# Masked sums of the encoder with the total taken out of row 0 of the value tables, in three jobs instead of four

## The reference, cut to what matters

```
smask = (i[:, None] & i[None, :] == 0)          # 1024 x 1024, 0 or 1
scores = einsum('bhqd,bhkd->bhqk', q, k) * scale
scores = scores * smask                         # masked scores are 0, not -inf
a = softmax(scores, axis=-1)
att = einsum('bhqk,bhkd->bhqd', a, v)
h = _ln(h + att @ wo + bo_, g1, be1)
h = _ln(h + gelu(h @ w1 + b1_) @ w2 + b2_, g2, be2)
```

## Time and profile before

| What | Value |
|---|---|
| median of 3 runs | 1929.28 us |
| the profiled execution | 1931.52 us, span of its instructions 1929.7 us |
| busy: PE, DVE, ACT, POOL | 1637.2, 1410.2, 1199.9, 254.4 us |
| mean granted clock of TensorE | 0.94 |
| chain that ended last: PE, DVE, ACT, issue, DMA | 38, 11, 8, 5, 4% |
| of it: DMA emr<-sce (the read-back of the maxima) | 4% |

### The profile page before, as it was taken

The page is one execution under the profiler, slowest core; times in us unless marked ns, Lnnn a source line. Parts: engine busy times, 40 slices in busy tenths (PEclk is TensorE's granted clock), DMA queues, the critical chain, the costliest instruction groups (busy, mean ns, idle before and its releaser), DMA issues.

```text
span 1929.7 us, 67065 instructions
## 1 busy us (share of the span) xinstructions
PE 1637.2 (85%) x28905; PEld 908.7 (47%) x28905; DVE 1410.2 (73%) x3361; ACT 1199.9 (62%) x2142; POOL 254.4 (13%) x229
## 2 busy tenths in 40 slices
PE   2789999899857689898989888888889898988896
PEld 1123333233324355555556555555555555656554
DVE  7778888987668767676867768576767686776755
ACT  2047776677831466676766767666766676776652
POOL 1000000000010202020302112120302030301111
PEclk8569999999977799999999999999999999999998
DMA  6122102001023433325242432343333424243000
GB/s 150 25 51 80 39 3 51 2 3 27 1 57 78 120 89 74 87 66 133 54 119 53 126 73 82 67 118 68 74 98 81 108 54 119 54 133 66 6 8 17
DMA packets 152204, 130.83 MB, mean 68 GB/s; under 512 B 65013, under 2 KB 147381, under 8 KB 149893
## 3 DMA queue, kind: packets, MB, share of 16 engines
q1 hardware_dynamic: 134629, 125.75, 26.6%
q10 hardware_dynamic: 17280, 0.79, 0.6%
HBM read 79.25 MB, written 45.88 MB: 65 GB/s over the span
## 4 chain that ended last, share of the span: by engine, by line
PE 38%; DVE 11%; ACT 8%; issue 5%; DMA 4%; ACTq 1%; POOL 0%; POOLq 0%; DVEq 0%
PE pB L670 8%; PE pO L685 7%; PE pA L650 6%; PE pG L621 5%; PE pG L631 5%; DMA emr<-sce 4%; DVE mx L933 3%; ACT PB L795 3%; PE pG L566 2%; ACT VD L753 2%; ACT HT L708 1%; DVE bst L474 1%; PE pG L598 1%; PE pG L580 1%; PE pG L585 1%
## 5 line engine op out<-in xcount | busy, mean ns | idle before, releaser
L795 ACT ACTIVATE PB<-pB 128x512 f32<-128x512 f32 (+1 forms) x1496 | 838.2, 593 | 434.3 <-PE pB L670 413.3
L933 DVE TENSOR_REDUCE mx<-pA 128x1 f32<-128x512 f32 (+3 forms) x1000 | 635.6, 669 | 124.4 <-PE pA L650 123.0
L670 PE MATMUL pB<-QS,KS 85*32 85x256 bf16 (+3 forms) x11264 | 597.8, 283 | 65.3 <-ACT PB L795 45.0
L650 PE MATMUL pA<-KS,QS 82*32 82x256 bf16 (+2 forms) x8384 | 541.1, 311 | 70.6 <-DVE mx L933 40.1
L685 PE MATMUL pO<-PB,VD 128*32 128x128 f32 (+3 forms) x5632 | 456.7, 397 | 6.2 <-issue 4.3
L670 PEld LDWEIGHTS pB<-QS,KS 85*32 85x32 bf16 x11264 | 260.2, 97 | 341.3 <-ACT PB L795 239.1
L650 PEld LDWEIGHTS pA<-KS,QS 82*32 82x32 bf16 x8384 | 202.4, 97 | 295.4 <-DVE mx L933 119.6
L933 DVE TENSOR_REDUCE mxb<-pA 128x1 f32<-128x512 f32 x304 | 206.8, 680 | 9.4 <-PE pA L650 9.2
L497 POOL TENSOR_TENSOR rstd<-vareps,mhalf 128x4 f32<-128x4 f32 x68 | 69.1, 1016 | 1071.9 <-DVE vareps L483 1071.0
L685 PEld LDWEIGHTS pO<-PB,VD 128*32 128x32 f32 x5632 | 159.8, 111 | 37.5 <-issue 9.2
L621 PE MATMUL pG<-HT,wL 128*128 128x512 f32 x192 | 94.5, 615 | 27.6 <-ACT HT L708 25.1
(11 more groups left out here) (186 smaller groups left out, 1536.2 us busy)
## 6 DMA issues: line engine op xcount, KB each, us to landing
scq<-PQ SPq DMA_DIRECT2D x84, 384.0 KB, 3.5
QS<-scq SPq DMA_DIRECT2D x56, 576.0 KB
KS<-sck SPq DMA_DIRECT2D x84, 384.0 KB
sck<-PK SPq DMA_DIRECT2D x28, 384.0 KB, 5.1
wL<-in_wL SPq DMA_DIRECT2D x6, 576.0 KB, 4.9
QS<-mt SPq DMA_DIRECT2D x168, 8.0 KB, 2.1
rE<-in_rE SPq DMA_DIRECT2D x7, 256.0 KB, 12.0
emr<-sce SPq DMA_DIRECT2D x96, 4.0 KB, 1.8
```

The costliest lines, as they stand in the source:

```text
L650: ins = pe.matmul(pA[QT * hd:QT * (hd + 1), a.a_bank(half, n), at:at + width], QS[0:R_A, r // NR, head, r % NR * QT:(r % NR + 1) * QT], ro ...
L670: ins = pe.matmul(pB[32 * i:32 * (i + 1), a.b_bank(h, v), at:at + width], KS[0:R_B, head, k0:k0 + 32], allowed(QS[0:R_B, x, head, :], 3, k ...
L795: act.activation(PB[:, pos_, 0:st.cols], pB[:, a.b_bank(h, v), 0:st.cols], ACT.Exp).then_inc(a.b_exped, 1)
L933: v.tensor_reduce(dst[:, gs[0]:gs[-1] + 1, tl[0]:tl[-1] + 1:step], pA[:, a.a_bank(half, n), 0:len(gs) * len(tl) * st.width] .rearrange("p ...
```

## The change

Three things, in one program.

**The total.** Row 0 of `negm` is minus one in every column (0 shares no bit with any query). A new job `tt0` makes the total on PE once a half, one matmul of `ones` by `VU[:, 7]` of 128 columns; DVE takes it out of partition 0 of all eight tables of `VU` (one operation on 1 partition, 8 x 128 elements). The matmuls by `negm` then give the masked sums by themselves. The count columns, which don't change, get theirs at the start of the program.

**The jobs.** Three `vm` jobs, for tiles (0, 1, 2), (3, 4, 5) and (6, 7), of 12, 12 and 8 matmuls of 144 columns; on DVE 432, 432 and 288 elements.

**The slots.** A steps stand one slot later, AV bundles three slots behind their B step instead of two, and all job tables are written anew, the dense ones too. The first wait of encoder jobs for the end of the dense attention moves from `qk00` to `ht0`.

```diff
+VM_TILES = ((0, 1, 2), (3, 4, 5), (6, 7))
+NVM = len(VM_TILES)
-LAG = 2
-        self.period, self.lead = (82, 36) if sparse else (256, 74)
+        self.period, self.lead, lag = (82, 36, 3) if sparse else (256, 74, 2)
-A_SLOTS = [*range(9, 36), 37, 39, 40, 42, 43, 45, *range(48, 81)]
+A_SLOTS = [*range(10, 37), 38, 40, 41, 43, 44, 46, *range(49, 82)]
 SPARSE_JOBS = {
-    "pe": [(-82, "gh5"), (83, "vm0"), (84, "vm1"), (90, "ot0"), (90, "vm2"), (-72, "gd2"), (-151, "gx0"),
-         (97, "vm3"), (-67, "gh6"), (-63, "gh7"), (-59, "gd3"), (106, "ot1"), (188, "zt0"), (108, "ot2"),
+    "pe": [(-80, "gh5"), (-80, "gd2"), (84, "vm0"), (-155, "gx0"), (-66, "gh6"), (99, "vm1"), (-62, "gh7"),
+         (105, "vm2"), (187, "zt0"), (189, "zh00"), (107, "ot0"), (-55, "gd3"), (109, "ot1"), (109, "ot2"),
...
             if kind == "ht":
                 hw(pe, ready, x + 1, CB)
+                if a.sparse and half.off == 0 and x == 0:
+                    pe.wait_ge(A0.res, NC)
...
                     wait_early(pe, half)
-                    if half.off == 0:
-                        pe.wait_ge(A0.res, NC)
...
-            elif kind == "vm":
+            elif kind == "tt":
                 hw(pe, a.u_step, USTEPS, USTEPS)
                 pg_free(pe, a, half, name)
-                for i in range(4):
-                    pe.matmul(pG[32 * i:32 * (i + 1), bank, 0:2 * VT].rearrange("p (t w) -> p t w", t=2), ones[:, :],
-                              VU[:, NB - 1, :, :].rearrange("p h w -> p (h w)").unsqueeze(1).to_broadcast([P, 2, VT]),
-                              start=True, stop=False, tile_position=(0, 32 * i), skip_group_check=True)
-                for j in range(2):
+                pe.matmul(pG[0:32, bank, 0:D].rearrange("p (h d) -> p h d", d=HD), ones[:, :],
+                          VU[:, NB - 1, :, 0:HD], start=True, stop=True).then_inc(a.total_filled, 1)
+            elif kind == "vm":
+                hw(pe, a.total_taken, 1, 1)
+                pg_free(pe, a, half, name)
+                for j, t in enumerate(VM_TILES[x]):
                     for i in range(4):
                         ins = pe.matmul(pG[32 * i:32 * (i + 1), bank, j * VT:(j + 1) * VT], negm[:, 32 * i:32 * (i + 1)],
-                                        VU[:, NB - 1 - (2 * x + j), :, :].rearrange("p h w -> p (h w)"),
-                                        start=False, stop=(j == 1), tile_position=(0, 32 * i), skip_group_check=True)
+                                        VU[:, NB - 1 - t, :, :].rearrange("p h w -> p (h w)"),
+                                        start=True, stop=True, tile_position=(0, 32 * i))
...
+            elif kind == "tt":
+
+                hw(v, a.total_filled, 1, 1)
+                row = VU[0:1, :, :, 0:HD]
+                v.tensor_tensor(row, row, pG[0:1, a.bank[name], 0:D].rearrange("p (h d) -> p h d", d=HD)
+                                .unsqueeze(1).to_broadcast([1, NB, H, HD]), ALU.subtract).then_inc(a.total_taken, 1)
...
-                hw(v, a.vm_scaled, 2 * (xh + 1), NQ)
+                hw(v, a.vm_scaled, 2 + xh, NVM)
...
-                (half + -1).wait(g, a.vm_filled, NQ, NQ)
+                (half + -1).wait(g, a.vm_filled, NVM, NVM)
```

## The result

| | Before | After |
|---|---|---|
| median | 1929.89 us (1921.96 to 1942.2, 20 runs) | 1940.13 us (1925.01 to 2059.31, 20 runs) |
| the profiled execution, its span | 1931.52, 1929.7 us | 1933.87, 1932.1 us |
| busy: PE, DVE, ACT | 1637.2, 1410.2, 1199.9 us | 1636.7, 1431.4, 1199.5 us |
| mean granted clock of TensorE | 0.94 | 0.93 |

The ratio after to before is 1.0041, 95% interval 1.0023 to 1.006: slower by 0.4%. Forecast were 1902 us and, with 0.72, faster. The forecast was wrong, and the time is also above its range. One of the 20 runs of after (2059.31 us at a clock of 0.78) was in a slower state of the chip; it, two runs of e9 and one of e12 are left out of the ratios.

A forecast was written before the change was run, and what follows sets the result against it. PE bounds the encoder (88% busy) but idles 12.6 us a period, partly behind waits for em; -2.35 us a half, eleven times -26, and -1 for the last half give 1902 us; own range 1890 to 1916, 8 in 10 1873 to 1930.

The forecast's parts named there:

- The rest: Remaining changes, dense tables included: nothing each, +-3 us on the whole together.
- The rival for it: Other jobs' new slots in the tables decide the result, either sign: 1880 to 1935 us; chance 7%.
- A0 earlier: Start of the next half: A0 at 13.9 us after the loads start, against 17.5; -3.6 us a half.
- The clock: TensorE's clock around A0: a loss of 1.1 us a half against 1.0 before, so +0.1 us.
- the second rival: The stall only moves: PE waits at A0, clock falls every half, +1.9 us; 1923 to 1926 us; chance 15%.
- em3 late: Read-back of k = 3 lands late around slot 105, holding DVE and PE: 1938 to 1964 us; chance 13%.
- The matmuls: PE's `vm` jobs: 1.96 us of `ones` go a half, `tt0` adds 0.15.
- `tt0` on DVE: Slot 49: 1.2 to 1.3 us, hidden beside PE's `out1` matmuls; costs 1.2 us if that cover is lost.
- The encoder in sum: Eleven halves with a successor, -2.35 us each: -26 us.
- that sign of being wrong: A period shorter or longer at slots 30 to 60, where no change was expected.
- The last half: The half without a following A0: loses only its `ones`, -1 us.
- PE's busy time: Sign of being right: PE's busy time falls by 20 to 36 us.

The follow-up runs named there:

- e9: Changed kernel with the closing dense stage's FP4 FFN jobs back in the slots of the kernel before: 1919.8 us, ratio to before 0.9937.
- e12: e9 with job `v1` two or three slots earlier, ahead of the start of the key and query loads: 1934.52 us, ratio to before 1.0021.
- e2: Kernel before with all dense tables of the changed kernel, nothing else: 1943.27 us, ratio to before 1.0054.
- e1: Changed kernel with all dense tables of the kernel before: 1920.31 us, ratio to before 0.9945.
- e11: Changed kernel with all dense slots of the kernel before, run once more: 1922.06 us, ratio to before 0.9943.
- e13: e9 run again unchanged, beside e12: 1924.98 us, ratio to before 0.9969.
- e5: Changed kernel with `res0` ahead of `gm2` on DVE and silu pairs `gs0`/`gs1`, `gs2`/`gs3` side by side on ACT: 1933.74 us, ratio to before 0.9999.
- e0: The changed kernel itself, run a second time: 1936.72 us, ratio to before 1.003.
- e3: Changed kernel with the old sums (matmuls of `ones` in each `vm` job) in the new slots: 1951.14 us, ratio to before 1.0094.
- e6: Kernel before with the new sums in its old slots, with two `tt` jobs at slot 50: 1943.88 us, ratio to before 1.0067.

## Why the prediction was wrong, point by point

**The step that failed** is "The rest": "the dense tables: nothing each, +-3 us on the whole together, since in every slot the same work stands on the same engine". They cost about 20 us in the profiled execution and 10 to 20 in the medians: 10 in e2, 16 to 19 in e1 and e11, and 12 to 20 for the FFN's slots alone in e9 and e13. The reason I gave is not true. In the dense tables slots were off by up to 21 (`ge0` on DVE, 591 before and 570 after; the eight that I named was too little), and what an instruction costs on ACT depends on its neighbour: `gs2` three slots from `gs3`, and `gs0` three from `gs1`, are one more round of table loads each, and putting both pairs side by side again (e5) wins 7 to 9 us. The rest of the loss is in the FFN's slots too (e9), only in part traced to a job. The trace of before had the 1.28 us loads and the pairs in it, and the table of slots had them apart; I did not put the two together. The rival for it had 7%, and a range that ended at 1935.

**A0 earlier** (predicted -3.6 us a half, A0 at 13.9): the mechanism was right, the size half. A0 came at 15.6 against 17.5, -1.8. I had PE arrive early and wait 2 to 3 us there; it came late instead, held 1.3 to 2.0 us by ACT's `v1` in each half, and by single halts (below). e12 has A0 at 13.6 with PE waiting for the data, so the 13.9 was read well from the earlier trace rows; its medians show no gain from it.

**The clock** (+0.1, the second rival +1.9): right for A0, wrong for the period. In the 6.5 us behind A0 the clock is 1.00 in all eleven halves of after, and 0.90 on the mean in before: some 0.7 us a half won, where I had put the loss of before at 1.0. But PE waits elsewhere now. The time of a half that the lower clock costs (each stretch less the stretch times its clock, on the mean of eleven) falls from 2.0 to 0.1 us at slots 88 to 91, and rises from 0 to 1.0 at slots 60 to 65 and from 0.3 to 1.9 at slots 76 to 87, behind the wait for `v1`; with `v1` earlier (e12) it is 0.4 there. Over the whole half it is 4.1 us for 2.9 (4.6, 3.4 and 4.0 in e0, e1 and e9). I had priced the clock at one place only, and the stall did move, not to A0 but ahead of it. The second rival's mechanism is seen in four halves of e12. Its number has a slip: with +1.9 in place of +0.1, a half comes to -0.55 and not -0.45, which changes nothing.

**em3 late** (third rival, 13%): refuted. DVE waits for all `em` together 14.9 us in 23 waits, the longest 1.9. **The matmuls**: right, e3 puts 1.0 to 1.2 us a half on the net of `ones` and `tt0`, where I had 1.8. **`tt0` on DVE**: 1207 ns, predicted 1.2 to 1.3, and hidden in the new slots; the 1.2 us that I named for a lost cover is what e6 pays.

**The encoder in sum**: predicted -26, measured -21.4 in after, by several terms by slots: 5.3 us a half are won at slots 88 to 91, 2.0 lost at 72 to 83, where `v1` stands now, and 1.6 lost from 96 on. At slots 30 to 60, where I expected no change, the exponentials shift (2.5 us less at 50 to 55, 2.6 more at 56 to 59), but from 36 to 59 it is 0.2 us in all, so that sign of being wrong did not come. The ten traces above put the encoder's gain at some 20 us. **The last half** (-1): +6.6. **PE's busy time** (20 to 36 us less): unchanged; the 29 us more at a lower clock are of that size.

With the dense slots undone the change is what it was forecast to be in sign: 1920.31 and 1922.06 us in two series, 0.9945 and 0.9943, the best version here beside e9 (0.9937, 0.9969), from which these runs can't tell it. It is still not 1902: the end takes 7.6 us more than I had it, A0 and the clock some of the rest.

## What to carry to other kernels

When a change comes with a newly written table, price the whole table, stage by stage: look in it for operations that were neighbours and are not any more (here activations of the same kind on ACT), and for an instruction that now stands behind a waiting one. A wait taken away is only won if the next limit is not just behind it: compare when the engine would arrive with when its data do, and what the clock does behind the new wait. A price for the clock has to cover every place where the new order makes PE wait, not only the one that the change is about. Test the stages that a change "doesn't touch" first, by giving each its old order back; one such run found here what the trace of the encoder alone could not.

## What the runs showed of the hardware that I had not expected

PE can halt in the middle of a row of equal matmuls, with nothing that the profile shows to wait for. Of e13, timeline, one A step:

```profile
1005.49 1.15 SPq L1005 DMA_DIRECT2D KS<-sck  x3
...
1009.58 0.24 PE L638 MATMUL pA<-KS,QS 82*32 82x128 bf16 x3
...
1016.83 0.40 PE L638 MATMUL pA<-KS,QS 82*32 82x128 bf16 x5 [7.01 <-issue]
```

Three matmuls, 7.01 us of nothing, five more. The e13 trace has three such halts of 3.1 to 7.0 us (14.9 us together), after has one of 3.84 and e11 one of 7.55, and each ends 11.2 to 11.6 us after SP starts the 1.7 MB of keys and queries, shortly before that traffic falls. Over the sixteen traces of this document there are 19 such halts of more than 3 us in the encoder, and 18 of them end 11.1 to 11.7 us after that start (the other one at 8.4); before has two of 2.9 and 3.0 us, ending at 13.8 and 10.8. In six traces one of 3.6 to 3.8 us stands in the first half; the others come in other halves in each execution. The two profiles of one kernel, e9 and e13, are 17 us apart (1913.9 and 1930.9). That PE's instructions come late behind those loads would fit; no run here took it apart, and it was not tried. For reading such cases it means that one profiled execution is good to about 15 us in its sum (17 here, and 15.4 for after and e0). A single stretch can be far better, but has to be seen twice: from exponential 432 to 511 after and e0 take 90.4 and 90.5 us, e9 and e13 75.4 and 75.5; from 64 to 432 after and e0 take 297.3 and 300.8.
